# A two-stage attention mix on one Trainium2 core: units as one stream with three score slots, keys masked on GpSimd, and four unread products ahead of the first scores

## The reference, cut to what matters

```
q, k, v = split_heads(x @ Wq), split_heads(x @ Wk), split_heads(x @ Wv)   # 16 heads of 8
scores = einsum('bqd,bkd->bkq', q, k) / sqrt(128)
attn = softmax(scores, axis=-1)          # over the queries
out = einsum('bkq,bkv->bqv', attn, v)
z = l2_normalize(merge_heads(out) @ Wo)
z = l2_normalize(z @ Wff)
z = gelu(z)
```

## Time and profile before

| | |
|---|---|
| Median of 3 runs | 6548.77 us (6543.41 to 6562.14) |
| The profiled execution, its time | 6545.28 us |
| Its span, first to last instruction | 6543.5 us |
| PE busy | 5082.6 us, 78% |
| ACT busy | 4305.5 us, 66% |
| DVE busy | 3856.2 us, 59% |
| POOL busy | 2494.6 us, 38% |
| mean granted TensorE clock | 0.845 |

### The profile page before, as it was taken

How to read it: one execution, slowest core, us unless ns; L and a number is a source line. 1 busy time by engine, 2 the same in 40 slices (tenths; PEclk the granted TensorE clock), 3 DMA queues, 4 the chain that set the end, 5 groups by cost and what they waited for, 6 DMA issues and landing times. The chain is left out here.

```text
span 6543.5 us, 177007 instructions
## 1 busy us (share of the span) xinstructions
PE 5082.6 (78%) x69200; PEld 3250.3 (50%) x69200; DVE 3856.2 (59%) x6192; ACT 4305.5 (66%) x8847; POOL 2494.6 (38%) x963
## 2 busy tenths in 40 slices
PE   1000069999999999977777899999999998687688
PEld 0000046666666666633333566666666666343443
DVE  4555556666666666655555566666666665546844
ACT  4333347777777777749999677777777776456655
POOL 0000045555555555514444555555555654000000
PEclk6555589999999999976666899999999999667866
DMA  1000022222222222200000222222222221000000
GB/s 48 0 0 0 0 66 55 67 58 60 60 61 64 57 63 60 52 12 1 0 0 1 57 65 59 62 59 64 57 64 60 61 60 41 9 0 3 0 2 7
DMA packets 181302, 248.00 MB, mean 38 GB/s; under 512 B 52076, under 2 KB 80232, under 8 KB 180072
## 3 DMA queue, kind: packets, MB, share of 16 engines
q1 hardware_dynamic: 176264, 221.95, 13.7%
q10 hardware_dynamic: 4320, 15.73, 0.8%
HBM read 43.50 MB, written 5.24 MB: 7 GB/s over the span
## 5 line engine op out<-in xcount | busy, mean ns | idle before, releaser
L401 PE MATMUL PS<-arena 128*128 128x512 f32 x2304 | 1171.0, 604 | 25.8 <-ACT arena L763 17.3
L1070 POOL TENSOR_TENSOR arena<-arena 128x1024 f32<-128x1024 f32 x192 | 551.8, 2874 | 932.7 <-DVE arena L969 932.7
L1070 POOL TENSOR_TENSOR lns<-arena 128x1024 f32<-128x1024 f32 x192 | 543.1, 2828 | 653.5 <-DVE arena L969 640.2
L939 DVE TENSOR_REDUCE arena<-PS 128x16 f32<-128x1024 f32 x192 | 235.1, 1225 | 773.3 <-PE PS L428 773.3
L958 DVE TENSOR_REDUCE arena<-arena 128x32 f32<-128x2048 f32 x192 | 438.9, 2286 | 395.5 <-ACT arena L763 395.5
L1440 PE MATMUL PS<-arena 128*128 128x512 f32 x8 | 5.6, 862 | 803.4 <-DVE arena L1374 803.4
L765 ACT ACTIVATE arena<-PS 128x512 f32<-128x512 f32 x384 | 229.9, 599 | 561.6 <-PE PS L401 558.2
L1073 POOL TENSOR_TENSOR lnc<-arena 128x1024 f32<-128x1024 f32 x192 | 546.5, 2846 | 0.0
L455 PEld LDWEIGHTS PS<-arena 64*64 64x64 f32 x24576 | 472.7, 134 | 145.1 <-issue 137.4
L1073 POOL TENSOR_TENSOR arena<-arena 128x1024 f32<-128x1024 f32 x192 | 541.1, 2818 | 0.0
L762 ACT ACTIVATE arena<-PS 128x512 f32<-128x512 f32 x768 | 481.4, 627 | 66.1 <-PE PS L401 42.8
(11 more groups left out here) (263 smaller groups left out, 11468.3 us busy)
## 6 DMA issues: line engine op xcount, KB each, us to landing
arena<-arena SPq DMA_DIRECT2D x2880, 64.0 KB, 2.0
arena<-in_L_ffn_Wqkv ACTq DMA_DIRECT2D x30, 512.0 KB, 4.1
arena<-in_L_ffn_Wo SPq DMA_DIRECT2D x48, 128.0 KB, 2.8
scratch<-arena SPq DMA_DIRECT2D x4, 1024.0 KB, 4.7
arena<-scratch SPq DMA_DIRECT2D x4, 1024.0 KB, 7.8
arena<-in_L_ffn_W SPq DMA_DIRECT2D x12, 341.0 KB, 3.0
arena<-in_L_ffn_Wqkv SPq DMA_DIRECT2D x6, 512.0 KB, 4.8
arena<-in_ffn_scales SPq DMA_DIRECT2D x12, 128.0 KB, 3.2
```

What stands on the lines that cost most here:

```text
L401: pe.matmul(PS[:, QKV + bank, :], xs[uu % 2][:, par * P:(par + 1) * P], w, start=True, stop=True).then_inc(qkv_ready, 1)
L1070: pool.tensor_tensor(halves(heads(t2)), halves(heads(raws[par]))[:, :, ::-1, :], sine, ALU.mult)\
```

## The change

- The hardware loops go. Each engine's list is written out for UNITS_MIX = 64 units, counted through all batches, and nothing is drained at a batch's end.
- Three slots (RING) in place of two, for score banks (0 to 5), exponentials and sums. Two buffers each for q, the masked keys and the values, so a batch can be prepared while the one before is in work. The output bank is 6, and the projections take bank 7.
- TensorE keeps its order scores(u+2), heads(u), now across batches: scores(0) of the next batch comes ahead of heads(6) of this one. q and k of the next batch are projected in unit 2, its values in unit 4, from XN itself; the copy to `hd_x` is gone.
- VectorE starts with shift(0) and shift(1), and then runs shift(u+2), values(u) where it was shift(u+1), values(u). The maximum is written negated, and the scale has moved into the copy of q, so the small product L1762 is gone.
- The masks are made on GpSimd (`mix_gpsimd`), each the product of 128 x 256 keys with a column read over 256 positions.
- ScalarE: copies of k, q and v for the next batch stand after units 3 and 5, and the copy of the output after unit 0 of the next batch.
- In front of scores(0), TensorE does four products of 128 x 128 by 512 columns (the mean matrix with XN) into the output bank. Nobody reads them.

```diff
-        hd_e = [hd.take(4 * T).rearrange("p (h t q) -> p h t q", h=2, t=2) for _ in range(2)]
         hd_st = [hd.take(16) for _ in range(2)]
+        RING = 3
+        mx_e = [hd.take(4 * T).rearrange("p (h t q) -> p h t q", h=2, t=2) for _ in range(RING)]
+        mx_st = [hd.take(16) for _ in range(RING)]
+        mx_q = [hd.take(T) for _ in range(2)]
+        mx_m = [[hd.take(T) for _ in range(HEADS_IN_GROUP)] for _ in range(2)]
+        mx_v = [hd.take(2 * C).rearrange("p (t n) -> p t n", t=2) for _ in range(2)]
...
-                wait_alone(pe, hd_masked, (g + 1) * HEADS_IN_GROUP)
-                wait_alone(pe, hd_projected, (g + 1) * 3)
-                scores(0)
-                scores(1)
-                for u in range(PAIRS8):
-                    if u + 2 < PAIRS8:
-                        scores(u + 2)
-                    heads(u)
-                    if u == PAIRS8 - 3 and not final:
-                        project_tensor(pe, g + 1)
...
+            def project(b):
+                g = run * B + 1 + b
+                pe.wait_ge(hd_projected, g * 3)
+                x = XN[:, b * T:(b + 1) * T]
+                for k in range(2):
+                    last = pe.matmul(PS[:, MIX_PROJ, k * T:(k + 1) * T], hd_w[k], x, start=True, stop=True)
+                last.then_inc(hd_proj, 1)
+
+            def project_values(b):
+                g = run * B + 1 + b
+                pe.wait_ge(hd_projected, g * 3 + 2)
+                for t in range(2):
+                    x = XN[:, b * T + t * P:b * T + (t + 1) * P]
+                    last = pe.matmul(PS[:, MIX_PROJ, t * C:(t + 1) * C], x, hd_w[2], start=True, stop=True)
+                last.then_inc(hd_proj, 1)
+
+            def scores(u):
+                b, n = divmod(u, PAIRS8)
+                g = run * B + 1 + b
+                if n == 0:
+                    pe.wait_ge(hd_masked, (g + 1) * HEADS_IN_GROUP)
+                    pe.wait_ge(hd_projected, g * 3 + 2)
+                if u >= RING:
+                    pe.wait_ge(hd_exp, first + u - RING + 1)
+                for t in range(2):
+                    for s in range(2):
+                        grp, v = head_of(n, s)
+                        rows = slice(grp * GROUP, (grp + 1) * GROUP)
+                        last = pe.matmul(score_banks(u)[:, s, t, :], mx_m[b % 2][v][rows, t * P:(t + 1) * P],
+                                         mx_q[b % 2][rows, :], start=True, stop=True)
+                last.then_inc(hd_scores, 1)
+
+            def heads(u):
+                b, n = divmod(u, PAIRS8)
+                if n == 0:
+                    pe.wait_ge(hd_copied, run * B + 1 + b)
+                pe.wait_ge(hd_v_ready, first + u + 1)
+                for t in range(2):
+                    for s in range(2):
+                        grp, v = head_of(n, s)
+                        at = grp * VGROUP + v * GROUP
+                        last = pe.matmul(PS[grp * GROUP:(grp + 1) * GROUP, MIX_OUT, 0:T], hd_vm[:, t, at:at + GROUP],
+                                         mx_e[u % RING][:, s, t, :], start=(v == 0 and t == 0),
+                                         stop=(v == HEADS_IN_GROUP - 1 and t == 1), skip_group_check=True)
+                last.then_inc(hd_out, 1)
+            pe.wait_ge(ln_scaled, (n0 + 1) * NCH)
+            project(0)
+            project_values(0)
+            for k in range(4):
+                pe.matmul(PS[:, MIX_OUT, :], mean_w[:], XN[:, k * CH:(k + 1) * CH], start=True, stop=True)
+            scores(0)
+            scores(1)
+            for u in range(UNITS_MIX):
+                b, n = divmod(u, PAIRS8)
+                if n == 2 and b + 1 < B:
+                    project(b + 1)
+                if n == 4 and b + 1 < B:
+                    project_values(b + 1)
+                if u + 2 < UNITS_MIX:
+                    scores(u + 2)
+                heads(u)
...
+            def copy_keys(b):
+                g = run * B + 1 + b
                 act.wait_ge(hd_proj, g * 2 + 1)
-                act.wait_ge(hd_scores, g * PAIRS8)
-                act.activation(hd_q, PS[:, 5, 0:T], ACT.Copy).then_inc(hd_projected, 1)
                 act.wait_ge(hd_masked, g * HEADS_IN_GROUP)
-                act.activation(hd_k, PS[:, 5, T:2 * T], ACT.Copy).then_inc(hd_projected, 1)
+                act.activation(hd_k, PS[:, MIX_PROJ, T:2 * T], ACT.Copy).then_inc(hd_projected, 1)
+                act.wait_ge(hd_scores, (g - 1) * PAIRS8)
+                act.activation(mx_q[b % 2], PS[:, MIX_PROJ, 0:T], ACT.Identity, scale=MIX_SCALE).then_inc(hd_projected, 1)
+
+            def copy_values(b):
+                g = run * B + 1 + b
                 act.wait_ge(hd_proj, g * 2 + 2)
-                act.wait_ge(hd_v_ready, g * PAIRS8)
-                act.activation(hd_v, PS[:, 6, 0:2 * C].rearrange("p (t n) -> p t n", t=2), ACT.Copy)\
+                act.wait_ge(hd_v_ready, (g - 1) * PAIRS8)
+                act.activation(mx_v[b % 2], PS[:, MIX_PROJ, 0:2 * C].rearrange("p (t n) -> p t n", t=2), ACT.Copy)\
                    .then_inc(hd_projected, 1)
 
-            def batch(g, b, final):
-                if not final:
-                    project_scalar(act, g + 1, b + 1)
-                for u in range(PAIRS8):
-                    act.wait_ge(hd_bias, nth(g, PAIRS8, u))
-                    if u >= 2:
-                        act.wait_ge(hd_out, nth(g, PAIRS8, u - 2))
-                    for s in range(2):
-                        for t in range(2):
-                            st = hd_st[u % 2]
-                            last = act.activation(hd_e[u % 2][:, s, t, :], PS[:, (u % 2) * 2 + s, t * T:(t + 1) * T],
-                                                  ACT.Exp, bias=st[:, 4 + 2 * s + t:5 + 2 * s + t], scale=MIX_SCALE,
-                                                  accum_out=st[:, 8 + 2 * s + t:9 + 2 * s + t])
-                    last.then_inc(hd_exp, 1)
-                if not final:
-                    copy_projected(g + 1)
-                act.wait_ge(hd_out, (g + 1) * PAIRS8)
-                act.activation(hd_Z[:, ds(b * T, T)], PS[:, 4, 0:T], ACT.Copy).then_inc(hd_copied, 1)
-            project_scalar(act, run * B + 1, 0)
-            copy_projected(run * B + 1)
-            with act.Fori(0, B - 1) as b:
-                batch(run * B + b + 1, b, False)
-            batch(run * B + B, B - 1, True)
+            def copy_out(b):
+                act.wait_ge(hd_out, first + (b + 1) * PAIRS8)
+                act.activation(hd_Z[:, b * T:(b + 1) * T], PS[:, MIX_OUT, 0:T], ACT.Copy).then_inc(hd_copied, 1)
+
+            def exps(u):
+                st = mx_st[u % RING]
+                act.wait_ge(hd_bias, first + u + 1)
+                if u >= RING:
+                    act.wait_ge(hd_out, first + u - RING + 1)
+                for s in range(2):
+                    for t in range(2):
+                        k = 2 * s + t
+                        last = act.activation(mx_e[u % RING][:, s, t, :], score_banks(u)[:, s, t, :], ACT.Exp,
+                                              bias=st[:, k:k + 1], scale=1.0, accum_out=st[:, 4 + k:5 + k])
+                last.then_inc(hd_exp, 1)
+            copy_keys(0)
+            copy_values(0)
+            for u in range(UNITS_MIX):
+                b, n = divmod(u, PAIRS8)
+                exps(u)
+                if n == 0 and b > 0:
+                    copy_out(b - 1)
+                if n == 3 and b + 1 < B:
+                    copy_keys(b + 1)
+                if n == 5 and b + 1 < B:
+                    copy_values(b + 1)
+            copy_out(B - 1)
...
-                shift(0)
-                for u in range(PAIRS8):
-                    if u + 1 < PAIRS8:
-                        shift(u + 1)
-                    values(u)
-                if not final:
-                    mask_vector(dve, g + 1, hd_k, 2)
...
+            def shift(u):
+                dve.wait_ge(hd_scores, first + u + 1)
+                dve.tensor_reduce(mx_st[u % RING][:, 0:4], PS[:, 2 * (u % RING):2 * (u % RING) + 2, :]
+                                  .rearrange("p h (t q) -> p (h t) q", t=2), AX_X, ALU.max, negate=True).then_inc(hd_bias, 1)
+
+            def values(u):
+                b, n = divmod(u, PAIRS8)
+                grp, v = head_of(n, 0)
+                st = mx_st[u % RING]
+                dve.wait_ge(hd_exp, first + u + 1)
+                dve.reciprocal(st[:, 8:12], st[:, 4:8]).then_inc(hd_recip, 1)
+                if n == 0:
+                    dve.wait_ge(hd_projected, (run * B + 2 + b) * 3)
+                dve.wait_ge(hd_out, first + u - PAIRS8 + 1)
+                dve.wait_ge(hd_recip, first + u + 1)
+                to = hd_vm[:, :, grp * VGROUP:(grp + 2) * VGROUP].rearrange("p t (h x) -> p t h x", h=2)                    [:, :, :, v * 40:v * 40 + 8]
+                fr = mx_v[b % 2][:, :, grp * GROUP:(grp + 2) * GROUP].rearrange("p t (h x) -> p t h x", h=2)                    [:, :, :, v * 8:v * 8 + 8]
```

(67 more changed lines are left out.)

28 lines of the change are left out of this document (1 added, 27 removed).

## The result

The changed kernel takes 6783.77 us (median of 4, 6775.35 to 6787.2) where the kernel before takes 6553.88 in the same comparison (6543.41 to 6562.14). The ratio is 1.035, 95% interval 1.033 to 1.037. The forecast was 6769 in a range of 6680 to 6805, with 0.84 on slower.

The account below looks back on a forecast made before the run. TensorE, back to back and mostly at low clock, was taken to bound the two mix streams. Two streams of 362 less 509.7 us, starts +4.4 and tails +2 gave +220.7: 6766, on the median 6769, range 6680 to 6805.

Parts of the forecast that it names:

- The closed chain: In each unit, heads, scores, maximum, reciprocal and values, next heads would wait on each other in turn instead of overlapping.
- The period: Time of one chained unit in the mix streams: 5.69 us at low clock, 3.94 at full, against 3.86 before.
- The units 3.9 us apart: Sign expected in the profile: starts of successive scores about 3.9 us apart where the clock is at 1.00.
- The share of full clock: Time at full clock in each new stream: half of before's, 26 us, taking 11.5 us off.
- The stream: Each mix stream, first scores to last output copy: 362 us where 255 were.
- the projections: Projections for the next batch, inside the chain seven times a stream: 1.3 us a batch at full clock, 2.6 at low.
- The two ends: First scores to first heads 4.9 us, last two heads 3.65 us; with 61 periods they add 8.6 us a stream.
- The start: From the end of XN to the first scores: 7.3 us for 5.1, so +2.2 a stream, bounds +1.0 and +4.4.
- GpSimd's masks: Four masks of 0.7 us each would hide behind the unread products; POOL busy some 45 us more.
- The rule against the forecast: The skill's rule: TensorE kept busy without long gaps gets the fast clock, so the stream would stay at full clock.
- The clock holding: First rival: products raise the clock and dense bursts keep it through the streams; 6559 us, no measurable change, chance 0.09.
- The overlapping at full clock: Second rival: maximum off the chain, TensorE the limit at 2.12 us a unit; 6338 us, chance 0.07.

Follow-up runs that it names:

- e1: Changed kernel with VectorE's list put back to shift(u+1), values(u), all else kept: 6347.09 us, ratio 0.9692 to the kernel before.
- e4: Kernel before with only VectorE's list within a batch moved to shift(u+2), values(u): 6738.54 us, ratio 1.0285.
- e5: Changed kernel, still chained, with two unread full-size products a unit between scores(u+2) and heads(u): 6564.36 us, ratio 1.0023.
- e10: e7 with the masks made on VectorE in place of GpSimd: 6453.87 us, ratio 0.9853 to the kernel before.
- e2: Changed kernel without the four unread products ahead of the first scores: 6791.52 us, ratio 1.0357 to the kernel before.
- e3: Changed kernel with VectorE's list put back to shift(u+1), values(u) and without the four unread products: 6339.76 us, ratio 0.9672.
- e7: e3 with q and k of the next batch projected in unit 0 in place of unit 2: 6327.91 us, ratio 0.9656.
- e8: Kernel before with two unread products of 256 columns a unit between scores(u+2) and heads(u): 6532.79 us, ratio 0.9976.
- e11: e10 with the first projection back in unit 2: 6391.09 us, five executions from 6338.13 to 6427.0, ratio 0.9736.
- e12: e10 with the four unread products put back ahead of the first scores: 6340.65 us, ratio 0.9682 to the kernel before.

## Why the prediction was right, point by point

- **The closed chain** was right. e1 opens it by VectorE's list alone, e4 makes it in the kernel before by the same line.
- **The period** was forecast at 5.69 and 3.94 us; measured 5.63 (maximum to heads 1.66 for 1.71) and, held at full clock in e5, 3.82 (heads to scores 0.98 where 1.06 was taken from another order). The units 3.9 us apart that the changed kernel was to show at 1.00 don't occur in it: after the start its full clock never lasts a whole unit, and its shortest ones take 4.1 to 4.2.
- **The share of full clock** was a guess at half of before's, 26 us a stream. The trace of the changed kernel has 23 and 25, so the guess was good, and a guess all the same. What it was to give back was not: 11.5 us stood in the sum, and against units of 5.63 the two streams have 7 and 8. Part of the time at full clock (6 and 4 us) lies ahead of the first heads, where it shortens no unit.
- **The stream** was forecast at 362 and measured 369.6 and 368.2, 13.8 short in all. Two terms are mis-sized, by some 4 us a stream each: what the full clock gives back, as just said, and the projections: 2.6 us a batch at low clock stood in the sum, and the sequence of heads, projection, scores adds 2.01 for the keys and 1.15 for the values (a unit with either took 7.64 or 6.79). The two ends came to 9.4, not 8.6: 5.3 us from scores to heads, 4.07 at the end. Against this stands a period 0.06 us too long, 3.7 us over 61 units, so the stream is as close as it is partly because errors offset each other.
- **The start** was forecast at +2.2 a stream and measured at +5.1 and +3.7. What was missed is a wait that the change adds: the projection of the values goes into the bank of q and k and waits for both copies, 0.75 us. And the products took 6.17 and 4.50 us, not 4.6 each.
- **GpSimd's masks** hide behind the products, as forecast: 0.61 us each where 0.7 was estimated, so GpSimd has 38 us more in all and not 45.
- **The rule against the forecast**, that a busy TensorE without long gaps gets full clock: in the middle of the changed stream the clock was at 1.00 and fell to 0.50 with no wait but one of 1.71 us, and e10's first stream stayed at 0.50 for 264 us with no gap at all. Neither goes with the rule in the Trainium skill, "TensorE: Matmul & The Clock Gate", section "Why this matters for your kernels". The fall at the changed stream's beginning says less about it, for the wait of 3.33 us ahead of the first heads is there too.
- **The rivals.** The clock holding was not to be had from the four products (e2 has the same time without them); e5 shows what it would have given. The overlapping at full clock, 6338 in the forecast at 0.07, is what the edit would have been with one line otherwise: e1 and e3 stand at 6347 and 6340.

## What to carry to other kernels

When two engines' instruction lists are written out by hand, look for the circle: write both lists one under the other and follow, for unit u, what each engine must have finished before it. Running an engine further ahead is no gain by itself; placed in front of the work that feeds the other engine, it turns two overlapping engines into one chain. Where the clock is the bound, a gap costs twice: its own length, and the clock of the work around it; and before trusting a version whose stretches begin at low clock, compare several executions, for one may sit at half speed from end to end.

## What the runs showed of the hardware that was not expected

Two stable speeds of one stream. With TensorE never waiting, a unit takes 3.86 us at 1.2 GHz and 2.05 us at 2.4, and either goes on by itself: 264 us at 0.50 and 145 us at 0.99 in e10, in one execution, with the same instructions. The rise stands behind full-size products (the projection in unit 2 in e3, in unit 0 in e7, the fillers in e5 and e8), but the projections of seven batches brought none in e10's first stream. That stream rose only at its end, 264.3 us in, where heads follow each other with no scores between them. Why the masks' engine matters, so that e10 and e11 stick and, by their times, none of e3's and e7's executions did, wasn't settled: with GpSimd's masks TensorE waits 1.1 us ahead of the first scores (e3, e7) and with VectorE's it doesn't, and whether that or another difference decides was not tried. e7's lead over e12 rests on five executions that, by their times, all rose early.
